# A transformer block in eight batches: the first batches and the last one arranged anew

## The chip, the cores and the metric

The kernel runs on one core of one Trainium2 chip. The metric is the device time of one execution in microseconds, taken as the median of three runs.

## The reference

One block of a conditioned transformer, 8 batches of 512 tokens by 256 features, 16 heads of 16:

```python
c6 = silu(c) @ Wc + bc                       # six rows of 256 for each batch: shift, scale, gate, twice
xm = ln(x) * (1 + sc_msa) + sh_msa
q, k, v = xm @ Wq + bq, xm @ Wk + bk, xm @ Wv + bv
w = softmax((q / 16) @ k.T)                  # for each head, over 512 keys
x = x + g_msa * ((w @ v) @ Wo + bo)
xm2 = ln(x) * (1 + sc_mlp) + sh_mlp
x = x + g_mlp * (gelu(xm2 @ W1 + b1) @ W2 + b2)   # 256 -> 1024 -> 256
```

## The kernel before

The kernel writes every wait and every order by hand; each engine has one program of steps i = -2 to 8 (`schedule`), and step i works on four batches at once: attention of batch i (`has_c`), the row maxima of batch i+1 (`has_b`), the first layer norm and the q, k, v products of batch i+2 (`has_a`), and the MLP of batch i-1 (`has_mlp`). Steps -2 and -1 have no attention, steps -2 to 0 no MLP, step 7 no later batch, and step 8 only the MLP of batch 7.

**Precision by splitting.** Projections are three fp32r products of a high and a low part (`three`, L601): the normed input z is cast to zh (`z_hi`, L1009) and zl = z - zh (`z_lo`, L1014 on VectorE and L435 on GpSimd). ScalarE writes z from PSUM with shift and scale (`modulate`, L514). q and k are cut into three bf16 parts each: ScalarE writes the high one (L570), VectorE the middle one (L1075) and the remainder (L1081), GpSimd the low one (L479). They lie in `parts`, which lives in the buffer of `prob`, so a batch's attention cannot write `prob` before they are used.

**Stacks.** Scores take the parts as six slots of 16 rows (96 partitions) in `qst[par]` and `kst[par]`. SyncE writes the parts of each of the four pieces (q or k, feature half 0 or 1) to DRAM (`write_parts`, L350, three DMAs a piece) and reads each piece back as a stack (`load_stack`, L356, 768 KB). Two more rows hold minus ones in kst and the row maximum, in two bf16 pieces, in qst.

**Row maxima.** A softmax needs its row maximum first. TensorE computes 64 blocks of scores a batch (`scores`, L664), VectorE takes the maximum of each (`row_max`, L995), TensorE turns them (`turn_maxima`, L682), VectorE makes two pieces (`maxima_rows`, L1018), and SyncE loads them into qst (`load_maxima`, L329). `max_banks` (L65) deals PSUM banks to blocks; MAX_FIRST serves batch 0 (banks 6, 7, 0, 1 for its first 34 blocks), MAX_SECOND batch 1 (6 and 7 in its tail), MAX_STEADY the rest. The blocks of batch i+1 lie between the products of step i by the tables in L53 to L61; in step -1, 34 blocks of batch 0 follow the q, k, v products, half the heads' maxima are loaded, and the rest of the blocks is done in step 0's attention, with 40 of batch 1.

**Attention.** 16 steps s of four heads: transposed scores, two exponentials on ScalarE (L550), and the product with v (`pv`, L692). The sums come with y; y goes to DRAM, the denominators come back, are inverted (L1091), written, and read back spread out as rb (L345 to L378); `y_norm` (L1101) multiplies and splits y, `wo_products` (L812) projects, `residual` (L1119) adds, and the second layer norm follows in the next step between row maxima.

**MLP.** `up(j)` (L838, six products into bank 4 or 5), gelu on ScalarE (L591), hh on VectorE (L1140), hl on GpSimd (L489), `down(j)` (L861, twelve products), for j = 0 to 7, up running three ahead.

**Start and end.** Weights are staged in `qst[1]` and `kst[1]`, Wc in `vaug[0]` and `qst[0]`. VectorE splits Wq, Wk and Wv, Wo (`split_weights`, L971), ScalarE and GpSimd the MLP weights (L579, L420). The x of batch 1 is loaded into the one buffer xa, when batch 0 has left it (L317). In step 7 attention comes alone; then the second layer norm of batch 6, its MLP, and among its j the projection of batch 7 (`WO_AT` = 2) and its layer norm (`LN2_AT`, `TURN_AT` = 5); step 8 is the MLP of batch 7 and one output DMA.

Each engine takes its instructions in order, so a wait holds what stands behind it on that engine.

## Time and profile before

| | us |
|---|---|
| median of 3 runs (734.41 to 738.68) | 735.15 |
| the profiled execution | 736.59 |
| its span, first to last instruction | 734.8 |
| TensorE busy | 684.5 (93%) |
| VectorE busy | 553.6 (75%) |
| ScalarE busy | 390.6 (53%) |
| GpSimd busy | 233.3 (32%) |

The mean granted clock of TensorE is 0.944 of full. Busy times are sums of instructions; a TensorE instruction's end is modelled. The rows that follow the change give starts from the first instruction. In rows, PE is TensorE, PEld its weight load, DVE VectorE, ACT ScalarE, POOL GpSimd, SP SyncE (SPq its DMA issues), and L12 is line 12 of the kernel before.

### The profile page before, as it was taken

Reading aid. Unit: us, or ns where it says so; the run is one execution under the profiler, and the core shown is the slowest. Engines: PE = TensorE matmul, PEld = TensorE weight load, DVE = VectorE, ACT = ScalarE, POOL = GpSimd, SP = SyncE. Lnnn points to the kernel's source line nnn. Section 1 sums busy time; section 2 is a strip of 40 time slices with the busy share of each in tenths; the row PEclk is TensorE's granted clock in tenths of the full one; section 3 lists DMA queues with packets and bytes.
Section 4 is the critical chain, followed back from the end, with each engine's and each line's share of the span. In section 5 each row is a group of like instructions: output and inputs, shape, how many; then the busy total and the mean of one; then the engine's idle time right before and its main releaser. Section 6 shows DMA issues by size and latency. Waiting matters only on the chain.

```text
span 734.8 us, 15491 instructions
## 1 busy us (share of the span) xinstructions
PE 684.5 (93%) x6409; PEld 415.3 (57%) x6409; DVE 553.6 (75%) x1012; ACT 390.6 (53%) x463; POOL 233.3 (32%) x169
## 2 busy tenths in 40 slices
PE   4788999869999999999999999999999989998986
PEld 2551333424478635874488447864587437724876
DVE  4769789868986898779887898689877985612553
ACT  5420457308862686348752885268634872497121
POOL 1446002201344132630363134413262123331344
PEclk8875699959999999999999999999999999999998
DMA  9589200591049301952177304930294111021010
GB/s 300 183 244 294 67 17 31 200 249 59 31 149 263 112 31 65 284 144 64 40 241 166 117 30 163 248 112 31 79 282 108 69 34 58 31 74 62 30 37 29
DMA packets 59858, 88.67 MB, mean 121 GB/s; under 512 B 6246, under 2 KB 47740, under 8 KB 56716
## 3 DMA queue, kind: packets, MB, share of 16 engines
q1 hardware_dynamic: 59788, 87.69, 39.5%
q8 instruction: 50, 0.82, 0.5%
q14 instruction: 20, 0.16, 0.1%
HBM read 49.35 MB, written 38.06 MB: 119 GB/s over the span
## 4 chain that ended last, share of the span: by engine, by line
PE 75%; DVE 12%; DMA 4%; ACT 3%; issue 3%; SPq 2%; POOL 1%; ACTq 0%; DVEq 0%
PE ps L649 22%; PE ps L702 13%; PE ps L604 13%; PE ps L854 7%; DVE mx L1007 6%; PE ps L655 6%; PE ps L785 4%; PE ps L858 3%; ACT prob L550 2%; PE ps L641 2%; PE ps L790 2%; PE ps L820 1%; DMA qst<-mrow 1%; DMA xa<-in_x_dram 1%; PE ps L830 1%
## 5 line engine op out<-in xcount | busy, mean ns | idle before, releaser
L1007 DVE TENSOR_REDUCE mx<-ps 128x1 f32<-128x512 f32 x512 | 330.7, 684 | 52.7 <-PE ps L655 30.8
L550 ACT ACTIVATE prob<-ps 128x1024 f32<-128x1024 f32 x256 | 248.2, 1024 | 129.9 <-PE ps L655 75.9
L649 PE MATMUL ps<-qst,kst 98*32 98x512 bf16 x1920 | 146.2, 383 | 1.8 <-ACT prob L550 1.8
L702 PE MATMUL ps<-prob,vaug 128*32 128x512 f32 x1024 | 135.7, 601 | 1.2 <-ACT prob L550 0.6
L649 PE MATMUL ps<-kst,qst 96*32 96x512 bf16 x1336 | 130.7, 389 | 1.4 <-DVE mx L1007 0.6
L489 POOL TENSOR_TENSOR hl<-z,hh 128x512 fp32r<-128x512 f32 x64 | 82.3, 1287 | 130.3 <-DVE hh L1140 130.3
L591 ACT ACTIVATE z<-ps,bias_t 128x512 f32<-128x512 f32 x64 | 44.0, 687 | 126.1 <-PE ps L858 119.4
L649 PEld LDWEIGHTS ps<-qst,kst 98*32 98x32 bf16 x1920 | 54.5, 98 | 77.1 <-issue 28.4
L655 PE MATMUL ps<-kst,qst 96*128 96x512 bf16 x178 | 72.6, 444 | 9.6 <-DVE mx L1007 9.5
L649 PEld LDWEIGHTS ps<-kst,qst 96*32 96x32 bf16 x1336 | 37.7, 95 | 73.0 <-DVE mx L1007 40.0
L604 PE MATMUL ps<-w_hi,hh 128*128 128x256 f32 x256 | 74.6, 292 | 0.3 <-POOL hl L489 0.2
L433 POOL TENSOR_TENSOR rstd<-vare,mhalf 128x4 f32<-128x4 f32 x16 | 16.7, 1046 | 175.1 <-DVE vare L934 175.1
L604 PE MATMUL ps<-w_lo,hh 128*128 128x256 f32 x256 | 72.3, 282 | 0.0
L604 PE MATMUL ps<-w_hi,hl 128*128 128x256 f32 x256 | 72.3, 282 | 0.0
L854 PE MATMUL ps<-zh,w_hi 128*128 128x512 f32 x128 | 60.4, 472 | 2.0 <-DVE zh L1012 2.0
L1140 DVE CAST hh<-z 128x512 fp32r<-128x512 f32 x64 | 36.2, 567 | 34.2 <-ACT z L591 34.2
L479 POOL TENSOR_TENSOR prob<-prob 128x512 bf16<-128x512 f32 x32 | 38.1, 1199 | 69.4 <-DVE prob L1081 68.2
L854 PE MATMUL ps<-zh,w_lo 128*128 128x512 f32 x128 | 50.9, 398 | 0.0
L604 PEld LDWEIGHTS ps<-w_hi,hh 128*128 128x128 f32 x256 | 48.7, 190 | 2.7 <-POOL hl L489 1.2
L604 PEld LDWEIGHTS ps<-w_lo,hh 128*128 128x128 f32 x256 | 48.5, 190 | 1.6
L604 PEld LDWEIGHTS ps<-w_hi,hl 128*128 128x128 f32 x256 | 48.5, 190 | 0.0
L702 PEld LDWEIGHTS ps<-prob,vaug 128*32 128x32 f32 x1024 | 31.3, 111 | 27.9 <-issue 9.9
(110 smaller groups left out, 908.8 us busy)
## 6 DMA issues: line engine op xcount, KB each, us to landing
parts_scratch<-prob SPq DMA_DIRECT2D x32, 384.0 KB, 3.0
qst<-parts_scratch SPq DMA_DIRECT2D x16, 768.0 KB, 9.4
kst<-parts_scratch SPq DMA_DIRECT2D x16, 768.0 KB, 14.3
parts_scratch<-prob SPq DMA_DIRECT2D x32, 256.0 KB, 3.1
y_scratch<-rb SPq DMA_DIRECT2D x32, 256.0 KB, 2.0
xa<-in_x_dram SPq DMA_DIRECT2D x8, 512.0 KB, 4.9
parts_scratch<-prob SPq DMA_DIRECT2D x32, 128.0 KB, 2.9
xd<-in_x_dram SPq DMA_DIRECT2D x8, 512.0 KB, 3.9
```

What stands on the lines that cost most here:

```text
L479: pool.tensor_tensor(parts[:, j, PART_AT[j // 2][2], :], rest[:, j % 2, :], parts[:, j, 1, :], ALU.subtract).then_inc(part_l, 1)
L489: pool.tensor_tensor(hl[:, j % HR, :], hb[:, j % HB, :], hh[:, j % HR, :].bitcast(F32), ALU.subtract).then_inc(hl_done, 1)
L550: act.activation(prob[:, s % 2, 2 * p:2 * p + 2, :], ps[:, 2 * p:2 * p + 2, :], ACT.Exp, scale=1.0 / DH).then_inc(exp_done, 1)
L591: act.activation(hb[:, j % HB, :], ps[:, 4 + j % 2, :], ACT.Gelu, bias=b1_t[:, j:j + 1]).then_inc(gelu_done, 1)
L604: m = pe.matmul(out_, a, b, start=start and n == 0, stop=stop and n == 2, skip_group_check=True)
L649: m = pe.matmul(out[32 * n:32 * n + 32, :], weights[:, 32 * n:32 * n + 32], moving, start=True, stop=True, skip_group_check=True)
L655: return pe.matmul(out, weights, moving, start=True, stop=True)
L702: m = pe.matmul(ps[32 * q:32 * q + 32, 4 + g % 2, :], vaug[par][:, kt, G * g + q, :], prob[:, s % 2, q, :], start=kt == 0, stop=kt == TT - ...
L785: pe.matmul(ps[:, QK_BANKS[2 * w + m], :], wqkvo[n][:, w, k, m * P:(m + 1) * P], zh[0][:, k, :], start=k == 0 and n == 0, stop=False)
L854: pe.matmul(ps[:, 4 + j % 2, :], w1[n][:, k, f], zh_of(1, b)[:, k, :], start=k == 0 and n == 0, stop=False)
L1007: dve.tensor_reduce(mx[:, t, h:h + 1], ps[:, banks[n], :], AXX, ALU.max).then_inc(max_done, 1)
L1140: dve.tensor_copy(hh[:, j % HR, :], hb[:, j % HB, :]).then_inc(hh_done, 1)
```

## The change

What it does, in order of the program:

- **Stacks from SBUF, all batches.** The DRAM buffer of the parts is gone. `fill_stack` issues, for each piece, one DMA of 128 KB for each of its six slots, from `parts` (128 partitions) into 16 rows of the stack (a stride of six partitions): 24 DMAs a batch, each sent as soon as its part is there. The row of a feature in the stack is changed alike for q and k. The pieces come in the order q0, k0, q1, k1 (`ORDER`), in all batches; TensorE's product order and VectorE's splits follow, and the reciprocal stands one piece earlier.
- **Start.** Wc's second half is staged in `vaug[1]`; x of batch 1 is loaded into x1 early (`xb_loaded`) and normalised there. ScalarE makes the high part of Wv and Wo, and GpSimd the low part; ScalarE's copies of W1 and W2 stand behind the second and fourth piece of batch 0, GpSimd's low parts of them (in halves) ahead of the pieces of batch 1. The rows of minus ones of kst[1] are copied by DMA. For batches 0 to 2 ScalarE writes zh from PSUM as well as z (`relieved`); for batches 1 and 2 ScalarE writes q or k in full and GpSimd subtracts the high part (`spared`), where VectorE did.
- **Row maxima of batches 0 and 1.** 12 blocks of batch 0 lie among the q, k, v products of step -1 (`EARLY_*`), 8 blocks of batch 1 instead of 4 among those of step 0; batch 1's tail uses four banks. Each of the tail blocks of steps -1 and 0 is computed twice (`copy`, into bank 2, never read), and before those tails TensorE waits for the third piece. `idle` adds fp32 products of the identity that nobody reads: 10, 2, 3, 6 at the start, 10 before the first attention, 8 after the turned maxima of step 0. In step 0 the first transposed scores stand ahead of the projection.
- **End.** In step 7 the layer norm, modulation and split of batch 6 are done by VectorE inside the attention, as are evacuations of y (`last_evacuate`), and of the twelve products of up(0) and up(1) one stands in each of the steps s = 7 to 15, the rest behind. up uses banks 6, 7, 0, 1 and runs four ahead. y of batch 7 is finished in two halves: the denominators are copied SBUF to SBUF, and half 0 is normalised during attention. The residual goes in two halves, the layer norm at j = 5 (`LAST_NORM_AT`), the turn at j = 6. ScalarE writes zh of batch 7. Step 8 runs the high products of up(0) to up(2) before their low ones; gate, add and output go in two halves.

The core of the diff:

```diff
+STACKED = 2 * NSLOT * 16
+PART_SLOTS = (((0, 3, 5), (1, 4), (2,)), ((2, 4, 5), (1, 3), (0,)))
+ORDER = (0, 2, 1, 3)
+EARLY_FIRST, EARLY_TURN, EARLY_QK, EARLY_V = 2, (0, 2), (0, 2, 0, 2), (1, 1, 1, 1)
-MAX_SECOND = max_banks(*attention(NEW_BLOCKS), ((6, 7), NH * TT - sum(NEW_BLOCKS)))
+MAX_SECOND = max_banks(*attention(NEW_BLOCKS), ((6, 7, 0, 1), NH * TT - sum(NEW_BLOCKS)))
-WO_AT, LN2_AT, TURN_AT = 2, 5, 5
+IDLE_START, IDLE_ATTENTION = (10, 2, 3, 6), (10, 8)
+WO_AT, TURN_AT = 2, 6
+LAST_TURN_AT, LAST_UP_AT = 4, 7
+LAST_NORM_AT = 5
+LAST_UP_BANKS, LAST_LEAD = (6, 7, 0, 1), 4
...
+        def relieved(n, b):
+            return n == 0 and (at(b, 0) or at(b, 1) or at(b, 2)) or n == 1 and final(b)
+        def spared(b):
+            return at(b, 1) or at(b, 2)
...
+                def fill_stack(b, n, which=(0, 1, 2)):
+                    j = ORDER[n]
+                    w, m = divmod(j, KC)
+                    stack = (qst, kst)[w][par]
+                    for part in which:
+                        sp.wait_ge((part_h, part_m, part_l)[part], 4 * b + n + 1)
+                        for slot in PART_SLOTS[w][part]:
+                            sp.dma_start(stack[slot:MROW:NSLOT, 8 * m:8 * m + 8, :], parts[:, j, part, :]).then_inc(stack_loaded[m], 16)
...
+                if early(i) and later(i, 2, 1):
+                    pool.wait_ge(xn_done[0], 2)
+                    mlp_weights(0)
+                    pool.wait_ge(zl_done[0], 2)
+                    mlp_weights(1)
...
+                        if spared(b):
+                            pool.tensor_tensor(rest[:, n % 2, :], rest[:, n % 2, :], parts[:, j, 0, :], ALU.subtract).then_inc(rest_set, 1)
+                            pool.wait_ge(rest_set, 4 * (b - 1) + n + 1)
+                        pool.wait_ge(part_m, 4 * b + n + 1)
+                        pool.tensor_tensor(parts[:, j, 2, :], rest[:, n % 2, :], parts[:, j, 1, :], ALU.subtract).then_inc(part_l, 1)
...
+                        if spared(b):
+                            act.wait_ge(part_l, 4 * b + n - 1)
+                            act.activation(rest[:, n % 2, :], ps[:, QK_BANKS[n], :], ACT.Identity,
+                                           bias=bqk[:, j // 2, j % 2:j % 2 + 1]).then_inc(rest_done, 1)
+                        if at(b, 0) and n % 2:
+                            act.wait_ge(wmlp_loaded[n // 2], 16)
+                            act.activation(w_mlp_high[n // 2], mlp_stage[:, 2048 * (n // 2):2048 * (n // 2 + 1)], ACT.Copy).then_inc(mlp_split, 1)
...
+            def idle(products, bank):
+                for _ in range(products):
+                    pe.matmul(ps[:, bank, 0:P], ident[:], ident[:], start=True, stop=True)
...
-                    scores(i, par, HALF + 2)
+                    if has_b:
+                        pe.wait_ge(rest_done, 4 * b + 3)
+                        pe.wait_ge(part_m, 4 * b + 3)
+                    scores(i, par, HALF + 2 - block_at[0], whole, 2)
                     turn_maxima(i, 0, NH // 2, half_turned, 4)
-                    scores(i, par, EXTRA - 2)
+                    scores(i, par, EXTRA - 2, whole, 2)
+                    if has_b:
+                        idle(IDLE_ATTENTION[0], 2)
...
+                if final(i):
+                    for k in range(2 * TT + 1):
+                        norm_piece(1, i - 1, x1, k)
+                    last_modulate(i - 1)
+                    z_lo(1, i - 1)
+                    for g in range(2):
+                        last_evacuate(g)
+                    last_reciprocal(0)
+                    last_norm(0)
+                    for g in range(2, NG):
+                        last_evacuate(g)
```

## Rows read from the trace of the kernel before

**Rows 1.** The page's second part: TensorE's granted clock, 40 slices of 18.4 us.
```profile
PEclk8875699959999999999999999999999999999998
```

**Rows 2.** Windows: length, then PE, PEld, DVE, ACT, POOL busy, clock, DMA share, GB/s.
```profile
50.30:72.30 22.00, 19.25 (x40) 3.86 (x38) 21.84 (x38) 0.60 (x1) 17.11 (x5) 0.61 0.95 282
72.30:86.00 13.70, 12.51 (x80) 3.50 (x84) 8.91 (x14) 4.05 (x5) 0.00 (x0) 0.51 0.34 98
86.00:130.00 44.00, 41.84 (x573) 15.82 (x566) 39.56 (x72) 29.48 (x33) 4.10 (x3) 0.96 0.06 20
142.40:155.30 12.90, 9.83 (x17) 1.74 (x17) 12.05 (x19) 0.00 (x0) 0.82 (x1) 0.56 0.90 275
207.10:286.40 79.30, 79.08 (x808) 50.88 (x808) 66.50 (x125) 47.87 (x58) 27.78 (x20) 1.00 0.44 132
638.50:670.80 32.30, 29.58 (x370) 8.64 (x370) 4.55 (x15) 29.62 (x34) 9.61 (x6) 1.00 0.19 64
685.30:703.00 17.70, 14.70 (x94) 13.17 (x93) 12.25 (x26) 2.49 (x4) 7.60 (x6) 0.92 0.01 1
710.20:729.00 18.80, 18.68 (x126) 17.16 (x126) 6.43 (x8) 4.13 (x6) 12.13 (x9) 1.00 0.07 22
```

**Rows 3.** The chain that ended last, 0 to 86: start, us, what.
```profile
13.84 8.02 DMA xa<-in_x_dram
...
31.11 1.12 DVE qst L962
32.23 3.17 DVE xa L942 x4
...
38.80 3.78 PE ps L785 x8
...
50.55 20.42 DVE mx L1007 x34
```

**Rows 4.** Timeline of ScalarE, then of VectorE, in the first 20 us.
```profile
19.80 0.69 ACT L570 ACTIVATE prob<-ps,bias_t 128x512 bf16<-128x512 f32 x1 [4.81 <-PE ps L790]
...
10.94 1.36 DVE L942 TENSOR_SCALAR xa<-xa,mv,rstd 128x256 f32<-128x256 f32 x4
```

**Rows 5.** Groups by line: busy us, mean ns, then idle before.
```profile
L479 POOL TENSOR_TENSOR prob<-prob 128x512 bf16<-128x512 f32 x32 | 38.1, 1199 | 69.4 <-DVE prob L1081 68.2
...
L1081 DVE SCALAR_TENSOR_TENSOR prob<-ps,bias_t,prob 128x512 f32<-128x512 f32 x32 | 23.8, 743 | 0.0
...
L425 POOL TENSOR_TENSOR w_lo<-kst,w_hi 128x2048 fp32r<-128x2048 f32 x1 | 4.5, 4507 | 0.0
```

**Rows 6.** The same chain, 128 to 168.
```profile
134.05 0.70 ACT prob L570
...
158.41 6.66 DMA qst<-mrow
```

**Rows 7.** The same chain, after 596.
```profile
676.21 3.40 DMA r_scratch<-rb
...
680.26 4.93 DMA rb<-r_scratch
...
717.58 0.93 PE ps L854 x4
...
718.97 1.43 PE ps L604 x12
```

**Rows 8.** The page's DMA issues: KB each, median us to landing.
```profile
parts_scratch<-prob SPq DMA_DIRECT2D x32, 128.0 KB, 2.9
...
kst<-parts_scratch SPq DMA_DIRECT2D x16, 768.0 KB, 14.3
```

**Rows 9.** SyncE's timeline, 274 to 345.
```profile
292.72 3.28 SPq L353 DMA_DIRECT2D parts_scratch<-prob  x6
```

**Rows 10.** The whole chain: the mrow load and the next attention, third iteration.
```profile
320.35 2.57 DMA qst<-mrow
...
325.92 1.42 PE ps L649 x24
```

More of the change, by code:

```diff
@@ L225, in dit_block @@
         o_done = sem("o_done")
+        last_half, last_normed = sem("last_half"), sem("last_normed")
+        last_den_loaded = [sem(f"last_den_loaded{k}") for k in range(KC)]
+        last_loaded = [sem(f"last_loaded{k}") for k in range(KC)]
         out_written = sem("out_written")
@@ L400, in step @@
                     load_maxima(qst[1 - par], 0, NH, m_loaded)
-                if runs(i, -1):
+                if final(i - 1):
+                    for n in range(2):
+                        rows = out[i - 1].rearrange("(t p) f -> p t f", p=P)
+                        sp.wait_ge(o_done, i + n)
+                        sp.dma_start(rows[:, 2 * n:2 * n + 2, :], osb[:, 2 * n:2 * n + 2, :]).then_inc(out_written, 16)
+                elif runs(i, -1):
                     sp.wait_ge(o_done, i)
@@ L662, in spare_free, with scores @@
                     pe.wait_ge(max_done, spare_used.pop(bank))
-            def scores(i, par, blocks, product=whole):
+            def scores(i, par, blocks, product=whole, copy=None):
                 banks, back = max_of(i + 1)
@@ L812, in wo_products @@
                 def wo_products(bank):
-                    pe.wait_ge(yh_done, i + 1)
+                    if not has_mlp:
+                        for p in range(2):
+                            first_transposed(i + 1, 1 - par, p)
+                    pe.wait_ge(yh_done, i + 2 if final(i) else i + 1)
                     for t in range(TT):
@@ L870, in down @@
                                       w2[0][:, j, :], w2[1][:, j, :], j == 0 and t % 2 == 0, j == JT - 1)
+                            if final(b) and j == JT - 1 and t == 1:
+                                m.then_inc(last_half, 1)
                         m.then_inc(w2_done, 1)
-                    for j in range(3):
-                        up(j)
-                        scores(i, par, UP_BLOCKS[j])
+                    lead = LAST_LEAD if final(i) or final(b) else 3
+                    if final(b):
+                        for which in (range(2 * KC), range(2 * KC, 3 * KC)):
+                            for j in range(3):
+                                up(j, which)
+                        up(3)
+                    else:
+                        for j in range(2 if final(i) else 0, lead):
+                            up(j)
+                            if not final(i):
+                                scores(i, par, UP_BLOCKS[j])
                     for j in range(JT):
@@ L1087, in step @@
+                for n in range(4):
+                    if n == 3:
+                        row_max(i, qk_blocks(i)[3] + sum(v_blocks(i)[0:2]))
                     if has_a:
-                        rest_of(i + 2, j)
-                    if j == 3 and has_c:
+                        rest_of(i + 2, n)
+                    if n == 2 and has_c and not final(i):
                         dve.wait_ge(den_loaded, 16 * (i + 1))
                         dve.reciprocal(rec, den).then_inc(rec_done, 1)
-                    if j < 3:
-                        row_max(i, others(QK_BLOCKS[j]))
@@ L1094, in step @@
[L1094 removed]
+                    if n < 3:
+                        row_max(i, qk_blocks(i)[n])
+                row_max(i, sum(v_blocks(i)[2:4]))
                 if has_a and not later(i, 2, 1):
+                    for t in range(TT):
+                        normalise(0, 1, x1, t)
                     add_c6(2, 512, (6, 7))
[L1097 to L1098 removed]
                     set_modulation(2, 4, 12, SC2)
@@ L1122, in residual @@
                     dve.wait_ge(xg_done, i + 1)
-                    if later(i, 0, 1) and not final(i):
+                    if later(i, 0, 1):
                         dve.wait_ge(o_done, i)
@@ L1148, in step @@
                             y_norm(j - 5)
-                        if final(i) and j == WO_AT:
-                            for part in range(3):
-                                y_norm(part)
-                        if final(i) and j == LN2_AT:
-                            residual(ps[:, 6:8, :])
+                        if final(i) and j == 1:
+                            last_reciprocal(1)
+                        if final(i) and j == 4:
+                            last_norm(1)
+                        if final(i) and j == LAST_NORM_AT:
+                            for n in range(2):
+                                last_residual(n)
                             for t in range(TT):
```

456 lines of the change are left out of this document (273 added, 183 removed).

## The prediction

> **What bounds the kernel now.** I read the clock line first, then windows by stage, then the chain, and last what single instructions cost. The middle is TensorE's: in the third iteration's window it is busy 79.08 of 79.30 us at full clock, VectorE 66.50 [rows 2]. Nothing there can be won unless products go, and none go. The clock line is below 9 tenths in its first five slices, in the ninth and in the last [rows 1]; there, and in the tail's gaps, TensorE waits, and there the change works, except that all batches get other stack loads. The first 20.42 us stretch of the chain is VectorE's, 34 row maxima at 0.60 us [rows 3]; the window round it has VectorE busy 21.84 of 22.00 [rows 2]. Behind it comes a start of attention at half clock (0.51, the lower level, 1.2 GHz), VectorE starved: 8.91 of 13.70 [rows 2]. Then attention is VectorE's again, 39.56 of 44.00. Batch 1's tail is VectorE's, 12.05 of 12.90, then 6.66 us go to a DMA of two small rows that stands behind 3 MB of stack loads [rows 2, 6]. In the tail ScalarE sets the last attention (29.62 of 32.30), then the chain goes through the denominators' DMAs (3.40 and 4.93 us) and the layer norm [rows 2, 7].
>
> **Part 1, up to the first maxima.** Now batch 1's x lands at 13.84 + 8.02 = 21.86, and VectorE does its statistics, Wv and Wo, and the splits of batch 0 only then; the norm ends at 35.4 and batch 1's first product starts at 38.80 [rows 3]. After the change x comes with the first loads and its statistics fit ahead of batch 0's first high part, which is at 19.80 today [rows 4] (0.6 earlier at best, since ScalarE writes zh; the ten idle products may win the clock too; I count neither). What is late next are the splits: four pairs at 2 x 0.66 us (0.743 with the read-out, [rows 5]) = 5.3 us, with ScalarE's 1.9 us copy of W1 in their middle (an estimate below half of GpSimd's 4.5 us for the same tile [rows 5]), so they end at about 26.5. The norm then takes between 1.36 us, as undisturbed, and 3.17, as beside GpSimd [rows 3, 4]; I take 2.3, and 1.1 for the sum with bc, as its row has it [rows 3]. With the turns the products of batch 1 start at about 33.3, 5.5 us sooner.
> From there a new chain decides, GpSimd's. Its low parts of W1 and W2 were 2 x 4.5 = 9.0 us under the maxima, where nobody waited. Now the second 4.5 us begins when batch 1's zl is there (36.5) and ends at 41; behind it, in order, stand the pieces of batch 1, two subtractions each, 2 x 1.2 = 2.4 us [rows 5]. ScalarE's write of the third piece waits for the first piece's low part, 43.5; VectorE's split of it is done at 45; TensorE waits for that before the tail of blocks. By then 6 of 34 blocks are done, and 6 more go with the fourth piece, until 49.2. The other 22 take 22 x 0.60 = 13.2: 62.4, against 50.55 + 20.42 = 70.97. That is 8.5. As four parts of the chain run beside VectorE's two-input work, I take 7.5. The first load of maxima is unchanged.
> **The price of the copies.** In these tails each block costs TensorE two products of 512 columns: 2 x 0.93 / 4 = 0.46 us at full clock, under VectorE's 0.60, or 2 x 3.78 / 8 = 0.94 at half clock, over it [rows 3, 7]. Today, with one product a block, the clock has a mean of 0.61 there and is at its lower level behind [rows 2]. No row shows whether 0.46 of 0.60 keeps it up. Ends: nothing, or 0.34 x 42 doubled blocks = 14 us if it never rises. At 0.94 TensorE would be busy without a gap, and such stretches do rise in this trace (86.00 on, 0.96 [rows 2]); so I count nothing.
> **Part 2, first attention.** If the clock is held, the 12.51 us of TensorE work in the window at 0.51 halve; VectorE then bounds at 8.91 instead of 13.70, 4.8 at most [rows 2]. The other end is nothing. I take 3.5.
> **Part 3, batch 2's splits and batch 1's tail.** From the first high part at 134.05 [rows 6] to the end of the maxima at 155.3 it is 21.3 us. VectorE now makes four of its eight splits: 22 blocks x 0.60 + 4 x 0.66 + 0.5 = 16.3, plus 1.4 until ScalarE's full copy and 0.9 where it waits for GpSimd's first pair: 18.6, so 2.7, of which 1.7 is the four banks (18 blocks in 12.9 us with the gaps at 0.7 before [rows 2], 0.60 behind). ScalarE's zh for the cast: 0.4. The fills are sent from DVE's first part on and their 24 x 128 KB are gone before the maxima; the load of maxima is then 2.6, as the third iteration has it [rows 10], instead of 6.66: 4.1. The turn at full clock: 0.4. Against it, the high products of the projection, which ran under that DMA, now stand behind the load: 1.8. Sum 5.8; ends 2 (load still late) and 8.
> **Middle.** SyncE issues 24 DMAs for 12 + 4. Six issues took 3.28, 0.55 each [rows 9], and 24 make 13 us at that price, beside products. Half of the bytes go. All must be landed at the next attention's first blocks of that batch, 325.92, 35 us after the first part; the old loads took 14.3 to land [rows 8, 10]. So 0 for the middle, ends -2 and +2, since TensorE has 0.2 us idle in 79.3.
> How many DMA engines a fill gets is what matters. The Trainium skill (DMA: Bandwidth & Descriptors, "Why a DMA increments its semaphore by 16 and not by 1") says a transfer is spread over the largest number up to 16 that divides the slowest dimension of both sides; here 128 and 16, so 16. By that rule a fill goes at the speed of these writes, and by that rule, the trace agrees for the old shape; no run here shows the new one.
> **Part 4, the tail.** The layer norm of batch 6 goes under attention, where VectorE has 4.55 of 32.30 [rows 2]: its work (about 8 us) fits. ScalarE loses three evacuations (0.4 each in the chain), 1.2, but TensorE, busy 29.58, gets nine products of 0.23 and a turn of 0.9; I call that equal (ends -1.2 and +2). After attention's last product (670.8) today come 58.1 us to the last product, of which 45.1 are 16 times one j, 717.58 to 718.97 + 1.43 = 2.82 [rows 7]. In the changed order I follow the engines: ScalarE's first gelu can end near 672, its low part near 674 (by 1.2 us for GpSimd as in L479 [rows 5]), and up(2) and up(3) cover until 673.6; then three times 2.82 to 682.5; the projection 2.9. Its input: y out of PSUM at 671.5, denominators by one small DMA (2.6, as the load of maxima [rows 10]), reciprocal 0.4, write 2.7 (at most 3.4), one half of the broadcast 3.0 (of 4.93 for two [rows 7]), multiply and split in three instructions of at most 0.74: 682, just hidden. Residual in halves, norm and root: 6.5 us beside 7.1 us of products; one us shows. Turn at 694, zh at 695.7 straight from ScalarE instead of z, zh, zl in line, and the nine high products of batch 7 cover zl; the first down starts at 702.2 instead of 710.2, where the last window begins. Its 18.8 us [rows 2] lose one up (1.4): last product at 719.6 instead of 729.0, 9.4. Halving the end, 2 x 1.24 to 2 x 0.62, gives 1.2; the half output 0.2. Sum 10.8. The window 685.30 to 703.00 shows where it was: TensorE 14.70 of 17.70. Ends: 7 (denominators not hidden, as 4.93 for a half too) and 13.
>
> **Sum.** 7.5 + 3.5 + 5.8 + 0 + 10.8 = 27.6 off the span of 734.8, 707.2; off the execution's own 736.6, 709.0. The median is 735.15, 1.4 below that execution, so 707.5.
>
> **Rivals.** (A) GpSimd is slower beside VectorE. The same four normalisations take 1.36 and 3.17 us [rows 3, 4], the slower ones while GpSimd ran. If each of the 8 + 2 operations of its chain in step -1 and of the 8 in step 0 gets 0.6 longer and the clock falls in a tail (22 x 0.13), parts 1 to 3 lose 3 + 2.9 + 2 and the tail 2: about 717. For: the chain has no slack. Against: row maxima read PSUM, and GpSimd's 17.11 us in the window at 50.30 left them at 0.60. The Trainium skill (GPSIMD Engine Reference, "1. Specifications") says GpSimd shares its SBUF interface with VectorE, contended by instructions with two SBUF inputs; by that rule the splits from PSUM are clear, and the trace agrees for the maxima.
> (B) The clock is held from the start and the gaps I left in are covered: part 1 gains 2.5 for the first products at full clock, part 2 1.3, the tail 1.5: 702.
> (C) Slower. The fills land late because rows go to 16 partitions only. The nearest slow row is the broadcast, 512 KB in 4.93 us, 104 GB/s [rows 7]; 3.1 MB take 30 us there, still inside 35. Batches 2 to 7 each lose what is over 35, so from 35 + 27.6 / 6 = 40 us a batch on (79 GB/s) the kernel is slower than before. At 60 GB/s it is 52 us and 707.5 + 6 x 17 = 810. Against: the writes of the same 128 KB from the same rows land in 2.9 us [rows 8], and half of the bytes are gone.
> (D) The doubled products stay at half clock and the denominators stay exposed: 14 + 3.5 + 4 given back, 729; with (A) it is no change.
>
> **Numbers.** My forecast 0.58, own range 703 to 712; (A) 0.18; (B) 0.12; (C) 0.04; (D) 0.08, of which 0.02 ends within 1%. The range of 8 in 10 leaves out (C), (D) and a part of (B): 701 to 719. About 1% is what a measurement here tells from no change: faster 0.94, same 0.02, slower 0.04.
>
> **What would show it.** Right: first long stretch of maxima ends near 62 to 64; no clock below 9 tenths after about 45 us; the load of maxima in step 0 under 3 us; the third iteration still 79.3 long; a single stretch of TensorE from 671 to the end less the layer norm of about 3 us. Wrong: a wait of VectorE or TensorE on GpSimd's L479 line over 3 us in step -1; clock 0.5 in the tails; scores waiting for stack loads in the middle, which would undo everything; ScalarE's exponentials further apart than 0.98 in the last attention.

## The result and the profile after

The changed kernel takes 717.57 us (median of four executions, 715.59 to 718.91), the kernel before beside it 735.73: ratio 0.9746, 95% interval 0.9704 to 0.9787. It is faster, as forecast, and inside the range of 701 to 719, but 10 us above the 707.5 forecast and outside that forecast's own range of 703 to 712. Its profiled execution has a span of 717.1 against 734.8.

First the page of the changed kernel: the clock line that answers to [rows 1], the end chain's engines, and the rows of the new stack fills.

```profile
PEclk9988999989999999999999999999999999999999
...
PE 81%; DVE 9%; issue 4%; ACT 3%; POOL 2%; DMA 1%; SPq 0%; ACTq 0%; DVEq 0%; POOLq 0%
...
qst<-prob SPq DMA_DIRECT2D x96, 128.0 KB, 3.3
kst<-prob SPq DMA_DIRECT2D x96, 128.0 KB, 3.4
```

The first slices now have 9, 9, 8, 8 tenths, and one slice near 145 to 160 us is still below 9. Each fill of 128 KB lands 3.3 or 3.4 us after its issue in the median; the old loads into kst, six times as large each, took 14.3 in the median [rows 8].

In rows from here on L is a line of the kernel shown. In the changed kernel L754 is a block of scores or the first transposed scores, L748 a score product made in pieces of 32 columns, L803 the product with v, L701 an idle product (two records each), L740 a turn, L972 and L980 the projection's high and low products, L857 a product of up, L694 one of `three`, in the tail of down, L1156 a row maximum, L494 GpSimd's low part of an MLP weight, L563 its first subtraction of a split; in the edited kernels the same lines stand up to fourteen lines off.

The longest pieces of the changed kernel's chain up to the second step of the second attention (start, duration, what):

```profile
33.57 1.24 DVE zl L1168
34.87 2.93 POOL w_lo L494 x2
...
39.57 1.17 POOL prob L563
...
45.31 1.94 PE ps L754 x5
47.25 4.89 PE ps L754 x11
52.16 9.12 DVE mx L1156 x15
63.23 3.59 PE ps L754 x8
66.82 3.58 PE ps L701 x20
71.65 1.30 DVE mx L1156 x2
...
118.64 1.04 PE ps L740 x8
...
133.53 9.58 DVE mx L1156 x16
143.76 1.79 PE ps L701 x16
145.54 3.08 issue
148.63 1.87 PE ps L754 x4
150.49 3.42 PE ps L972 x16
153.91 1.43 PE ps L980 x8
155.34 1.42 PE ps L748 x21
```

GpSimd's W2 at 34.87 and its first pair of splits at 39.57 stand in line, as forecast. The first maxima end at 61.3 (70.97 before). Then come blocks and idle products until 70.4, and only then scores. After the second tail TensorE waits 3.08 us, and the three rows behind run at half clock. The windows (columns as in [rows 2]) show the same:

```profile
47.00:61.00 14.00, 13.40 (x47) 4.30 (x46) 13.84 (x24) 0.00 (x0) 3.71 (x4) 0.80 0.47 137
61.00:72.00 11.00, 9.54 (x44) 5.35 (x42) 5.85 (x10) 1.04 (x2) 0.00 (x0) 0.69 0.36 109
143.00:156.00 13.00, 9.77 (x64) 8.17 (x68) 5.51 (x9) 1.95 (x2) 0.00 (x0) 0.74 0.44 116
196.00:276.00 80.00, 79.79 (x812) 51.53 (x811) 66.98 (x125) 47.84 (x58) 27.84 (x20) 1.00 0.31 93
```

Between 61 and 72 us VectorE is busy 5.85 of 11.00 us and TensorE 9.54, at a mean clock of 0.69: the engine that paces attention is starved, while TensorE works through doubled blocks and idle products. The middle is as before, TensorE 79.79 of 80.00.

The chain of the tail:

```profile
627.04 1.24 DVE x L1329
...
635.42 1.09 PE ps L740 x8
...
660.55 1.12 PE ps L857 x4
661.67 0.99 PE ps L803 x8
662.66 2.98 PE ps L857 x12
...
693.67 1.39 POOL hl L575
695.11 1.69 PE ps L694 x12
```

The denominators' DMAs, 8.3 us of [rows 7], are gone from it. Stage by stage, each length from one landmark to the next (the 34th maximum, attention's last product with v, L702 or L803, and the last product of all, 728.92 and 712.40, count by their end, the others by their start; gains are taken before rounding):

| stage | before | after | gain | forecast |
|---|---|---|---|---|
| start to the 34th maximum | 71.0 | 61.3 | 9.7 | 7.5 |
| from there to batch 2's turn | 56.9 | 57.4 | -0.4 | 3.5 |
| turn to the next attention's second step | 39.2 | 36.7 | 2.5 | 5.8 |
| to x of the last attention | 471.4 | 471.7 | -0.3 | 0 |
| to that attention's last product | 32.2 | 35.6 | -3.4 | 0 |
| to the last product | 58.1 | 49.7 | 8.4 | 9.4 |
| to the end | 5.9 | 4.7 | 1.2 | 1.4 |

The gains add to 17.7, the forecast was 27.6. Three stages carry the miss: the second, third and fifth.

### The profile page after: what moved, and what is told of

The parts are those of the page before. It is cut to its first block, busy times and chain, and to the rows that moved or that the text cites. A ratio compares the mean times of both kernels' runs of the same rounds, so it can differ in the third digit from the quotient of the medians.

```text
span 717.1 us, 15858 instructions
## 1 busy us (share of the span) xinstructions
PE 684.7 (95%) x6529; PEld 423.7 (59%) x6529; DVE 550.9 (77%) x1006; ACT 398.0 (56%) x474; POOL 237.2 (33%) x179
## 4 chain that ended last, share of the span: by engine, by line
PE 81%; DVE 9%; issue 4%; ACT 3%; POOL 2%; DMA 1%; SPq 0%; ACTq 0%; DVEq 0%; POOLq 0%
PE ps L748 23%; PE ps L694 14%; PE ps L803 14%; PE ps L857 12%; PE ps L754 6%; DVE mx L1156 5%; PE ps L933 3%; PE ps L972 2%; PE ps L740 2%; PE ps L701 2%; PE ps L938 1%; PE ps L980 1%; ACT prob L635 1%; ACT z L613 1%; ACT zh L613 1%
## 5 line engine op out<-in xcount | busy, mean ns | idle before, releaser
L1156 DVE TENSOR_REDUCE mx<-ps 128x1 f32<-128x512 f32 x512 | 330.9, 685 | 53.8 <-PE ps L754 33.0
L748 PE MATMUL ps<-qst,kst 98*32 98x512 bf16 x1920 | 143.2, 379 | 0.6 <-ACT prob L635 0.6
L803 PE MATMUL ps<-prob,vaug 128*32 128x512 f32 x1024 | 134.8, 597 | 0.7 <-DVE x L1329 0.4
L748 PE MATMUL ps<-kst,qst 96*32 96x512 bf16 x1336 | 129.0, 383 | 1.9 <-DVE mx L1156 1.0
L748 PEld LDWEIGHTS ps<-qst,kst 98*32 98x32 bf16 x1920 | 53.8, 97 | 68.7 <-issue 27.4
L754 PE MATMUL ps<-kst,qst 96*128 96x512 bf16 x220 | 73.6, 413 | 8.1 <-DVE mx L1156 7.5
L748 PEld LDWEIGHTS ps<-kst,qst 96*32 96x32 bf16 x1336 | 37.5, 95 | 72.0 <-DVE mx L1156 39.6
L694 PE MATMUL ps<-w_hi,hh 128*128 128x256 f32 x256 | 74.2, 290 | 2.5 <-POOL hl L575 2.5
L694 PE MATMUL ps<-w_hi,hl 128*128 128x256 f32 x256 | 72.1, 281 | 0.0
L694 PE MATMUL ps<-w_lo,hh 128*128 128x256 f32 x256 | 72.0, 281 | 0.0
L857 PE MATMUL ps<-zh,w_hi 128*128 128x512 f32 x128 | 60.6, 473 | 0.0
L1344 DVE CAST hh<-z 128x512 fp32r<-128x512 f32 x64 | 36.7, 575 | 30.8 <-ACT z L681 23.6
L857 PE MATMUL ps<-zh,w_lo 128*128 128x512 f32 x128 | 51.2, 400 | 0.0
L694 PEld LDWEIGHTS ps<-w_hi,hh 128*128 128x128 f32 x256 | 48.3, 189 | 4.9 <-POOL hl L575 3.4
L694 PEld LDWEIGHTS ps<-w_lo,hh 128*128 128x128 f32 x256 | 48.2, 188 | 1.6
L694 PEld LDWEIGHTS ps<-w_hi,hl 128*128 128x128 f32 x256 | 48.2, 188 | 0.0
L803 PEld LDWEIGHTS ps<-prob,vaug 128*32 128x32 f32 x1024 | 31.1, 110 | 26.4 <-issue 9.5
```

Of the source, the lines that this page charges most:

```text
L694: m = pe.matmul(out_, a, b, start=start and n == 0, stop=stop and n == 2, skip_group_check=True)
L748: m = pe.matmul(out[32 * n:32 * n + 32, :], weights[:, 32 * n:32 * n + 32], moving, start=True, stop=True, skip_group_check=True)
L754: return pe.matmul(out, weights, moving, start=True, stop=True)
L803: m = pe.matmul(ps[32 * q:32 * q + 32, 4 + g % 2, :], vaug[par][:, kt, G * g + q, :], prob[:, s % 2, q, :], start=kt == 0, stop=kt == TT - ...
L857: m = pe.matmul(ps[:, banks[j % len(banks)], :], w1[low_weights][:, k, f], (zl_of if low_norm else zh_of)(1, b)[:, k, :], start=n == 0, st ...
L1156: dve.tensor_reduce(mx[:, t, h:h + 1], ps[:, banks[n], :], AXX, ALU.max).then_inc(max_done, 1)
```

## The experiments

Each ran beside the kernel before; ratios are to it, so that chips don't matter. The stage lengths come from each one's profiled execution. The times are medians of four executions, five for the last. Letters: A from the end of batch 1's zl to the 34th maximum, B to batch 2's turn, C to the second step, D the middle, E last attention, F to the last product, G to the end. What stands ahead of A, the start up to zl, took 33.5 to 35.1 us and is touched by none of the edits.

| run | us | ratio, interval | A | B | C | D | E | F | G |
|---|---|---|---|---|---|---|---|---|---|
| changed kernel | 717.57 | 0.9746 [0.9704, 0.9787] | 26.4 | 57.4 | 36.7 | 471.7 | 35.6 | 49.7 | 4.7 |
| unchanged, again | 716.91 | 0.9758 [0.9724, 0.9793] | 26.5 | 57.4 | 37.2 | 471.5 | 35.6 | 49.7 | 4.7 |
| no idle before attention | 717.70 | 0.9727 [0.9675, 0.9779] | 26.1 | 51.6 | 35.8 | 473.7 | 35.6 | 49.7 | 4.7 |
| no copies | 716.01 | 0.9706 [0.9675, 0.9737] | 26.1 | 56.8 | 34.0 | 473.1 | 35.6 | 49.8 | 4.7 |
| no up products inside | 717.28 | 0.9728 [0.9695, 0.9761] | 26.1 | 55.3 | 37.5 | 471.7 | 33.0 | 52.5 | 4.7 |
| projection first | 713.90 | 0.9683 [0.9654, 0.9711] | 26.1 | 55.2 | 34.9 | 472.8 | 35.6 | 49.8 | 4.7 |
| splits back | 714.92 | 0.9724 [0.9691, 0.9758] | 24.8 | 55.3 | 37.5 | 473.4 | 35.6 | 49.7 | 4.7 |
| W2's low parts late | 715.19 | 0.9740 [0.9715, 0.9765] | 23.5 | 55.3 | 37.6 | 473.2 | 35.6 | 49.7 | 4.7 |
| turn one step later | 717.66 | 0.9774 [0.9741, 0.9806] | 26.4 | 57.4 | 36.9 | 473.1 | 35.7 | 49.7 | 4.6 |
| joined | 712.44 | 0.9674 [0.9639, 0.9708] | 23.5 | 55.5 | 34.4 | 473.7 | 35.6 | 49.9 | 4.1 |
| joined, no copies | 711.24 | 0.9668 [0.9638, 0.9699] | 23.5 | 55.5 | 33.4 | 474.2 | 35.6 | 49.9 | 4.1 |
| joined, splits back | 715.13 | 0.9711 [0.9681, 0.9742] | 24.8 | 55.6 | 34.0 | 474.2 | 35.6 | 49.9 | 4.0 |
| joined, no copies, sum later | 713.11 | 0.9675 [0.9648, 0.9702] | 23.5 | 55.3 | 33.8 | 473.8 | 35.6 | 50.8 | 4.1 |

**The idle products before the first attention.**

```diff
-IDLE_START, IDLE_ATTENTION = (10, 2, 3, 6), (10, 8)
+IDLE_START, IDLE_ATTENTION = (10, 2, 3, 6), (0, 8)
```

> The changed kernel without the 10 idle products ahead of the first attention. Theory (the idle products are themselves the delay: at half clock they take 3.6 us, 66.62 to 70.24, while the load of maxima has landed): the first scores start near 67 instead of 70.24, the layer norm's turn of batch 2 (118.64) comes 2 to 3 us sooner, the total is 2 to 3 us less. Rival (they buy their own price): the first scores start sooner but run at the lower clock until the products have raised it, the turn of batch 2 stays at 118 to 119.5, the total within 1 us.

In the profiled execution B is 5.8 us shorter without them: the first attention's scores came 5.3 us after the 34th maximum and not 10.0. Of the 5.8, some 3.6 are the idle products' own time; the rest is the clock, since B is 55.3 and 55.2, not 57.4, in two kernels below that have the changed kernel's instructions up to there (no up products inside, projection first). Its chain:

```profile
46.08 14.34 DVE mx L1156 x24
62.37 3.33 PE ps L754 x12
66.08 1.30 DVE mx L1156 x2
```

But the four executions took 713.39, 715.18, 720.58 and 720.23, so the median moved by nothing, as the rival had it for the total. The two slower ones have a mean clock of 0.979 and 0.980 against 0.987 and 0.989; where it was down in them no profile shows. In the joined version, which leaves the products out too, the clock was down at the start of attention, and B is 55.5, as in four kernels that have them (55.2 and 55.3). By the medians they cost what they save.

**The copies.** Each block of the two tails is made once (the last argument of three calls goes).

> The changed kernel with each block of the tails of steps -1 and 0 computed once; the idle products stay. Theory (the second product holds the clock and costs nothing where VectorE paces): the 34th maximum ends at 61 to 62 as now, the clock falls to its lower level near 52 instead of 62.6, the first attention starts at the lower level and loses 1 to 3 us, step 0's tail keeps 16 maxima in 9.6 to 10.5 us; total 1 to 4 us more. Rival (the copies cost as much as they hold): the six blocks in two banks go from 0.85 back to 0.60 each, 1.3 us less, and the total is within 1 us or less.

The windows of this kernel, its first maxima and what follows:

```profile
46.50:60.70 14.20, 13.21 (x26) 2.59 (x25) 14.20 (x25) 0.00 (x0) 4.04 (x5) 0.50 0.48 140
60.70:71.00 10.30, 8.47 (x38) 5.03 (x37) 5.68 (x10) 1.27 (x2) 0.00 (x0) 0.62 0.40 117
```

The clock is at its lower level, 0.50, for the whole tail and VectorE still has 14.20 of 14.20: A is 26.1, as in three kernels with the copies and a clock of 0.91 to 1.00 from 45 to 61 us, and 0.3 less than with the copies and 0.79 (26.4). One product of a block at half clock is 0.47 us, under VectorE's 0.60, so a copy can't help the maxima; it only takes TensorE's time in the six blocks behind them. The theory failed: B is no longer than with the copies. The ratio is 0.9706 against 0.9746 and 0.9758; the intervals overlap.

The larger gain stands in C, 34.0 against 36.7. The same products stand behind the load of maxima here, but the clock is down earlier, under the second tail, and up again when the load lands (0.99 from 147 to 152 us). A window, then rows of the chain:

```profile
137.00:147.00 10.00, 7.53 (x26) 4.43 (x25) 8.71 (x15) 0.00 (x0) 0.00 (x0) 0.50 0.67 183
...
147.60 1.02 PE ps L754 x4
148.62 1.89 PE ps L972 x16
```

With the eight low products (0.95) they take 3.9 us instead of the 6.7 in the changed kernel: that is what the new order costs at full clock, 1.9 more than the 2.0 of before.

**No up products inside the last attention.** They go back behind it.

```diff
-                        if final(i) and s >= LAST_UP_AT:
-                            up(divmod(s - LAST_UP_AT, 3 * KC)[0], (divmod(s - LAST_UP_AT, 3 * KC)[1],))
...
-                        for j in range(2 if final(i) else 0, lead):
+                        for j in range(lead):
```

> The changed kernel with all products of up(0) and up(1) behind the last attention, none in it. Theory (each product in the attention costs 0.30 of a step of 2.27, more than the 0.23 it takes alone, because the attention was TensorE's by then): steps go back to 1.97 to 2.0, attention ends 2.5 to 3 us sooner, the MLP behind needs 2.8 us more before its first gelu, total within 1 us of the changed kernel. Rival (ScalarE's attention hides them): steps stay near 2.27 without them, total 2 to 3 us more.

E falls by 2.6 and F rises by 2.8: the products are moved, not hidden. In the changed kernel's timeline of TensorE (start, duration, line, tiles) one of them sits between others so:

```profile
641.38 1.03 PE L803 MATMUL ps<-prob,vaug 128*32 128x512 f32 x8
642.34 0.50 PE L857 MATMUL ps<-zh,w_hi 128*128 128x512 f32 x1
642.77 1.05 PE L748 MATMUL ps<-qst,kst 98*32 98x512 bf16 x16
```

It holds TensorE for 0.43 us, 642.34 to 642.77; within a run of its kind such products follow at 0.23. A step then takes 2.27 and not 1.97 us, so the net price is 0.30 a product. ScalarE is idle 0.33 us in each step with one, and 0.18 in each second step without.

**The projection ahead of the first scores in step 0.** This is the order of before.

```diff
-                    if not has_mlp:
-                        for p in range(2):
-                            first_transposed(i + 1, 1 - par, p)
                     pe.wait_ge(yh_done, i + 2 if final(i) else i + 1)
...
-                    if has_mlp and not final(i):
+                    if not final(i):
+                        if not has_mlp:
+                            first_transposed(i + 1, 1 - par, 0)
                         first_transposed(i + 1, 1 - par, 1)
```

> The changed kernel with step 0's order of before: the 16 high products of the projection ahead of the first transposed scores. Theory (the order costs: TensorE stands idle 3.1 us under the load of maxima, its clock falls to the lower level, and the 24 products then take 4.85 us instead of 2.9): the products run in the idle time, the next attention's second step starts at 152 to 153 instead of 155.34, total 2 to 3 us less. Rival (ScalarE's first exponentials set it, so scores first is right): no gain, total within 1 us.

C falls from 36.7 to 34.9 and the time to 713.90, ratio 0.9683. It is the best single edit by the time; its interval meets that of the changed kernel at the edge (0.9704 to 0.9711) and lies clear of the unchanged one's. But C is as short without the copies (34.0), where the order is the changed kernel's: most of what the order costs is the half clock on the products behind the load. Its chain shows what ends last there now, the denominators' broadcast under the fills:

```profile
136.44 6.38 DMA rb<-r_scratch
142.91 1.24 DVE yc L1298
...
145.27 3.35 PE ps L969 x16
```

**The splits back on VectorE.**

```diff
         def spared(b):
-            return at(b, 1) or at(b, 2)
+            return False
```

(and VectorE waits for GpSimd's last low part of the batch before.)

> VectorE makes the middle and rest parts of batches 1 and 2 alone again (GpSimd keeps only the low parts, ScalarE only the high ones). That gives VectorE 4 x 0.66 = 2.6 us back in each of two steps where row maxima follow at 0.60 without a gap. My theory now: the chain ScalarE - GpSimd - ScalarE that replaced them made VectorE idle nearly as long (1.0 + 0.4 + 2.7 us of idle between 34.7 and 46.5), so the 34th maximum moves from 61.3 only to 62 to 63, and step 0 by as little; 718 to 720. The prediction's view: 2.6 us lost in each step, the 34th maximum at 64, and 722 or more. Rival that the contention of GpSimd and VectorE costs more than the splits save: 716 or less.

The maxima end sooner, not later: A is 24.8 against 26.4. The relief made its batch wait for W2's low parts on GpSimd, which cost more than it gave: 1.6 us by the trace, while the intervals of the times overlap. My theory had the size nearly and the sign wrong. The time is where the rival put it, but not for its cause: with W2's low parts out of the way (joined, splits back) the same edit makes A longer, so the contention costs less than the splits save.

**Nothing altered.**

> The changed kernel once more, nothing altered, as the measure for the others: 715.5 to 719. If where the clock falls is chance, the window from 45 to 61 us, at 0.79 in the first profile and 1.00 in two of the other kernels that are identical up to there, comes out different here, and the time of the first transposed scores after the idle products (71.65) moves to about 70.0 as in those two. If it comes from the code, it is 0.79 again and 71.6.

The clock in that window is 0.79 again and B 57.4 again. Executions of one kernel differ by their clock: in the first four its mean was 0.979 twice (spans 717.1 and 717.1) and 0.987 and 0.988 twice (714.5 and 713.8); here 0.979 to 0.989, 717.2 to 712.6. So B's 57.4 against 55.3 in the table tells executions apart, not kernels: the kernel without up products inside has the same instructions there, and 1.00 in that window. That the three profiles at 57.4 agree within 0.3 us in where the clock falls is not explained, and the runs here can't say why the fall sits where it does.

**W2's low parts behind batch 1's pieces.**

```diff
-                    pool.wait_ge(zl_done[0], 2)
-                    mlp_weights(1)
...
                     if early(i) and later(i, 2, 1):
+                        mlp_weights(1)
                         pool.wait_ge(c6_done, 2)
```

> GpSimd makes W2's low parts (4.7 us) behind batch 1's four pieces, not before them. My theory: GpSimd's chain in step -1 is what VectorE and TensorE stand behind (2.7 us of idle on VectorE, TensorE's wait before 44.2), so the 34th maximum ends 2.5 to 3.5 us sooner than 61.3, and the time is 714.5. Rival: SyncE sends batch 1's second to fourth piece only when the last low part is made, that is at about 51 and not 40; its 21 DMAs at 0.7 us each then end at 66 and the load of maxima (62.6 now) stands behind them: nothing gained, 717 to 720.

A is 23.5, 2.9 less, as my theory had it. The rival is half right: SyncE's queue of this kernel (start, duration) is full until the very moment of the load of maxima.

```profile
50.98 3.80 SPq L432 DMA_DIRECT2D kst<-prob  x6
54.82 3.81 SPq L432 DMA_DIRECT2D qst<-prob  x6
58.68 3.83 SPq L432 DMA_DIRECT2D kst<-prob  x6
62.55 1.43 SPq L389 DMA_DIRECT2D qst<-mrow  x2
```

Maxima are ready at 58.8 and their load is issued at 62.55. This execution hid that under the idle products; the middle then gave back 1.5 us (473.2 for 471.7), and the time, 715.19, is within the intervals of the unchanged kernel's.

**The turn one step later.** `LAST_TURN_AT` is 5 instead of 4.

> The turn of batch 6 in the last attention comes after step 5, not 4. My theory: at step 4 it waits for the norm (GpSimd's root 632.9, VectorE 634.3 to 635.4, TensorE's turn 635.42, and ScalarE idle 1.26 us before 637.11); one step later it waits for nothing, and the stretch from the last x of the norm's input to the end of attention (34.6 us) gets 1.0 to 1.9 shorter: 716. Rival: the first up product is due two steps later and its factors now come too late, so that what is won at the turn is lost at step 7: 717.5.

Nothing is won, E is 35.7. ScalarE's timeline in this kernel:

```profile
635.22 3.77 ACT L635 ACTIVATE prob<-ps 128x1024 f32<-128x1024 f32 x4 [0.18 <-PE ps L748]
640.31 3.77 ACT L635 ACTIVATE prob<-ps 128x1024 f32<-128x1024 f32 x4 [1.31 <-PE ps L748]
```

The 1.31 us gap is there although the turn waits for nobody. Its eight products take 1.02 us themselves between two score groups, and ScalarE has no stock of scores to live on. I had read the gap of 1.26 as the norm's wait; it is the turn's own length.

**Joined.** The projection first, no idle products, W2's low parts late, and three new edits, none of them run alone: batch 1's second q piece is filled before SyncE waits for the low parts; batch 6's gating stands ahead of batch 7's zl, its sum behind the first high part of batch 7's MLP; the last two down groups are made for rows 0 and 1 first.

```diff
                     if early(i) and later(i, 2, 1):
+                        fill_stack(i + 2, 2)
                         sp.wait_ge(low_split, 4)
...
+                            dve.wait_ge(w2_done, JT * i)
+                            dve.tensor_tensor(osb[:], ps[:, DOWN_BANK:DOWN_BANK + 2, :].rearrange("p n (t f) -> p (n t) f", t=2),
+                                              gm[:].unsqueeze(1).broadcast_to([P, TT, H]), ALU.mult).then_inc(o_gated, 1)
                             z_lo(1, i)
...
+                                for tiles in ((0, 1), (2, 3)):
+                                    down(j - 1, tiles)
+                                    down(j, tiles)
```

> Five edits joined: projection ahead of the first scores in step 0 (as in the fourth run), no idle products before the first attention (first run), W2's low parts behind batch 1's pieces (seventh run) with batch 1's second q piece sent ahead of the wait for them, batch 6's gating ahead of batch 7's zl and its sum behind the first high part of batch 7's MLP, and batch 7's last two down groups made for rows 0 and 1 first. Expected against 717 of the changed kernel: load of maxima issued right behind the maxima (at 59, not 62.5), first scores of the first attention at 64 to 65 (71.7 in the changed kernel, 66.9 in the seventh run); turn of batch 2 to the next attention's second step 34.9 (36.7); last product of batch 6's attention to the last product of all 0.7 shorter; from there to the end 0.5 shorter (5.4 now). Sum 7 + 1.8 + 1.2 = 10, less 1.5 for the later fall of the clock near 590: 708.5 to 711. Rival: the falls of the clock in steps -1 and 0 only move, and what is won ahead of them comes back behind them: 713 to 715.

712.44, ratio 0.9674: 1.4 us above the band and under the rival's. A, C and G came as expected (23.5, 34.4, 4.1), and so did the first scores (65.0), but B stayed at 55.5 and F at 49.9. In this execution the clock is at its lower level from the blocks ahead of the scores into the attention (62 to 72 us), and the middle took 473.7.

**Joined, each block once.**

> The joined version with each block of the two tails made once, not twice. If the copies hold nothing that counts (second run: maxima at 0.60 us with TensorE's clock at 0.50 as with 1.00), this is equal or up to 1.5 us faster than the joined version, because the six blocks in two banks take half of their products. If the copies keep the clock up for the first attention, it is 2 to 4 us slower: at half clock that attention's first 13 us took 13.7 in the kernel before [rows 2].

711.24, and the lowest ratio of all, 0.9668 [0.9638, 0.9699], though the joined version's interval overlaps it nearly whole. The copies keep nothing up that counts: B is the same 55.5. Of the 2.2 us between the two profiles 1.0 is in C; 1.6 lie ahead of zl, in code that is the same.

**Joined, splits back.**

> The joined version with VectorE making the splits of batches 1 and 2 alone. Alone this edit was worth 0 to 2 us (fifth run), because it took batch 1's pieces from behind W2's low parts on GpSimd. Theory: in the joined version these low parts are already behind, so the edit now costs what the prediction said of it, 2.6 us less waits in each step: 1 to 3 us slower than the joined version. Rival: the chain over two engines costs as much as it saves anywhere: equal within 1.

715.13, 2.7 more than joined (the intervals overlap), with 1.3 of it in A: with the low parts behind, the splits on two engines do pay, half of what the prediction said. In C the maxima end 1.2 us later too (25.7 us after the turn, 24.5 in the joined version), but it does not show in the sum, since the clock was down earlier and the projection's high products took 2.13 us instead of 2.79.

**Joined, no copies, the sum later.** The `j == 0` before batch 6's last sum becomes `j == 3`.

> The tenth kernel with one thing moved: batch 6's last sum (VectorE, 1.22 us, two inputs from SBUF) behind the fourth high part of batch 7's MLP, not the first. In the ninth run GpSimd's first low part took 2.17 us beside that sum, against a median of 1.28 and never over 1.38 in the changed kernel, and from the end of batch 6's attention to the first down product it took 32.6 us, as much as before the edit (32.45). If the two engines hindered each other there, the low part takes 1.3 us again and the first down product starts 0.8 to 0.9 us sooner (31.7), and the kernel takes 710.5. If the low part was long for another cause, it is 2.2 us here too and nothing changes: 711.2.

GpSimd's timeline in the joined kernel, its first low part of batch 7 (start, duration, line, tiles, idle time before and its releaser):

```profile
688.16 2.17 POOL L576 TENSOR_TENSOR hl<-z,hh 128x512 fp32r<-128x512 f32 x1 [6.38 <-DVE hh L1351]
```

The same engine's timeline in this last kernel:

```profile
686.99 1.28 POOL L576 TENSOR_TENSOR hl<-z,hh 128x512 fp32r<-128x512 f32 x1 [6.39 <-DVE hh L1351]
...
691.93 2.20 POOL L576 TENSOR_TENSOR hl<-z,hh 128x512 fp32r<-128x512 f32 x1 [0.36 <-DVE hh L1351]
...
697.48 0.74 POOL L532 TENSOR_TENSOR yc<-gm,b_b 128x256 f32<-128x256 f32 x1 [1.69 <-DMA gm<-c_scratch]
698.30 2.40 POOL L535 TENSOR_TENSOR xa<-xa,yc 128x1024 f32<-128x1024 f32 x1
```

The first low part takes 1.28 us now and the first down product starts 31.7 us after attention, 0.9 sooner, both as expected. The 2.2 us went with the sum, to the fourth low part. But F is 50.8, not the 49.0 that would follow: the output of batch 6 left later, behind it on SyncE the load of gm, and behind that load GpSimd's two additions for the last output, which end at 700.70; its next low part starts only then. The gain of 0.9 was given back twice.

## Why the prediction was right or wrong

**Part 1 was right in its chain, and its gain 2.2 larger than I took.** Batch 1's zl came at 34.8 (forecast 36.5), GpSimd's first piece, TensorE's wait until 44.2 (forecast 45) and the 34th maximum at 61.3 (forecast 62.4) all stand in the chain where they were put. From zl to the maxima it took 26.4, between my 25.9 and the 26.9 with the us taken off for GpSimd beside VectorE. What the step missed is that its own edit made this chain: with W2's low parts behind the pieces A is 2.9 shorter.

**The price of the copies, counted as nothing, was right for the maxima and for a reason I did not see.** I compared 0.46 and 0.94 us with 0.60, the two products of a doubled block. The single one at half clock is 0.47. So the change had nothing to win there, and rival (D)'s 14 us could only come from the copies.

**Part 2: the attention gained as forecast, and the wait in front of it took it back.** From its first scores to batch 2's turn it took 50.7 us before and 47.4 after, 3.3 against my 3.5. But from the 34th maximum to the first scores it now takes 10.0 us, 6.3 before. I had the idle products and the six blocks in two banks as cover for a wait, and left out what they cost when the clock is down: 3.6 us for eight products (four doubled blocks), 3.6 for the ten idle ones. The sum is -0.4. The kernel without those idle products has the scores 5.3 us behind the maximum.

**Part 3: the term for the projection was mis-sized.** The other terms held: from the first high part to the end of the maxima 18.4 us (forecast 18.6), and the load lands 5.5 us behind that, 9.8 before. ScalarE's zh gave nothing of its 0.4. But the products behind the load, which I put at 1.8 more, took 1.87 + 3.42 + 1.43 = 6.7 against 2.0: 4.7 more. I had priced them at full clock: at full clock, in the kernel without copies, they took 3.9, 1.9 more than before, and my 1.8 holds. The other 2.8 are the lower clock. That the 3.08 us wait in front of them lets the clock go is not shown: in the kernel with the splits back the clock went down (0.57 from 141.4 to 144.3) while TensorE was busy all of that time, ahead of its wait. The experiment with the old order gives 1.8 to 2.6 back, against the 36.7 to 37.5 of kernels with the change's.

**Middle: right.** 0.3 us lost, and fills that land in 3.4 us can't be late for rows due 35 us on, so rival (C) is out. I said 16 engines for a fill by a rule of the Trainium skill (DMA: Bandwidth & Descriptors, "Why a DMA increments its semaphore by 16 and not by 1"); by that rule a fill goes about like the old writes of the same size, and the trace agrees as far as the time goes, 3.3 and 3.4 us against 2.9 [rows 8].

**Part 4: "I call that equal" failed.** Attention takes 3.4 us more. Without the nine products E is 33.0, so they cost 2.6 of it, 0.30 a step; the other 0.8 is the turn (a gap of 1.3 us on ScalarE) less what the evacuations gave back, and no run parts the two. My own rows could have said so: 29.58 + 9 x 0.23 + 0.9 is 32.6 us for TensorE, over the 31.1 that ScalarE was to need. My end of the range was +2. Beside it F gained 8.4 of 9.4: the denominators were hidden, norm and turn ran as described. Of the missing 1.0 the last kernel places 0.75: VectorE's two output instructions of batch 6 stood ahead of batch 7's first high part, and with both elsewhere the first down product starts 31.7 us after attention and not 32.45. The halved end gave 1.2 of 1.4.

**The rivals.** The time fits (A), 717, but its mechanism did not occur: GpSimd's eight subtractions took 1.17 each, 0.6 less than it asks, and A is 0.5 over my steps, not 3 or more. So the agreement of the time with (A) is luck: three other terms add up to it. (B) did not come: even the execution at a clock of 0.988 has a span of 713.8. (D)'s two conditions are both refuted: the clock was 0.80 from 47 to 61 us and at its upper level in the second tail (1.00 from 130 to 148), and the denominators were hidden. Of my signs, "no clock below 9 tenths after about 45 us" failed, at 143 to 161 us above all; it pointed at the term of part 3.

## What to carry to other kernels

Filler work that is to keep an engine's clock up stands in the chain itself when the clock is down, and then costs double: before adding it, see whether the engine that bounds would notice the lower clock at all. A fall of the clock under row maxima cost nothing here where each block was made once (A 26.1), and on the products behind the load it cost 2.8 us. Products moved into a stage whose own engine has no stock cost their full length and more (0.30 us for one of 0.23); moving them is only a gain where a wait stands. When work goes to a helper engine, list its queue in order: what stood there unobserved (W2's low parts, an addition behind a load) becomes the bound.

## What was not expected of the hardware

GpSimd and VectorE hinder each other in a sharp way. The same subtraction from SBUF on GpSimd took 1.28 us in the median and at most 1.38 among 64 in the changed kernel, and 2.17 to 2.20 in the joined kernels, once in each profile, where VectorE added two SBUF tiles beside it. VectorE's cast of 0.43 us took up to 1.5 where that subtraction ran beside it, as here in the changed kernel (GpSimd's timeline, then VectorE's):

```profile
663.88 1.29 POOL L575 TENSOR_TENSOR hl<-z,hh 128x512 fp32r<-128x512 f32 x1 [21.89 <-DVE hh L1344]
...
663.95 1.50 DVE L1344 CAST hh<-z 128x512 fp32r<-128x512 f32 x1
```

In the changed kernel 25 of the 64 casts start while a GpSimd instruction runs, and each ends 0.28 to 0.30 us behind that instruction's end, however long the overlap: 0.74 us for 0.46 of it, 1.12 for 0.84, and 2.43 beside an addition of 2.41. So the cast's time is the rest of GpSimd's instruction and 0.28 us. Row maxima out of PSUM stayed at 0.60 beside GpSimd. The Trainium skill (GPSIMD Engine Reference, "1. Specifications") says that the two share an SBUF interface and that VectorE's instructions with two SBUF inputs, or in a 2-port mode, contend for it. By that rule the addition hinders the subtraction, and the trace agrees, also in that the maxima are clear of it; the cast has one SBUF input, so only the other half of the rule can bear on it, and no run here shows the cast's mode.

Where the clock falls is not fixed by the kernel: identical code up to 630 us had 0.79 from 45 to 61 us in three profiles and 1.00 in a fourth. In ten of the thirteen profiles another fall near 590 us lasted twice as long (6.8 to 6.9 us, not 3.4 to 3.5), and the middle took 472.8 to 474.2 us and not 471.5 to 471.7. I did not test what decides either; two or three us of each kernel's time hang on them, as much as the single edits above.
